# State scan of a two-layer model: y summed token-major by accumulating transposes, one eighth of u·B by PE with diagonal matrices from GpSimd

## The reference, cut to what matters

```
z       = second half of in_proj(hidden)          # 512 channels
delta   = softplus(...)                           # [token, d]
u       = delta * x_conv
h[t,d,n] = exp(delta[t,d] * A[d,n]) * h[t-1,d,n] + u[t,d] * B[t,n]
y[t,d]   = sum over n of h[t,d,n] * C[t,n]
y       = (y + x_conv * D) * silu(z)
out     = y @ out_proj.T                          # added to x
```

## Time and profile before

| | us |
|---|---|
| median of three runs | 1728.73 (1726.64 to 1728.74) |
| the profiled execution | 1728.79 |
| its span | 1727.0 |
| PE busy | 1649.3 (96%) |
| DVE busy | 1394.7 (81%) |
| ACT busy | 1267.8 (73%) |
| POOL busy | 765.0 (44%) |
| first product h·C to the end of the last, sequence 0 | 1140.15 to 1312.79 |
| the same, sequence 1 | 1386.29 to 1559.79 |

### The profile page before, as it was taken

The page is one execution under the profiler, slowest core; times in us unless marked ns, Lnnn a source line. Parts: engine busy times, 40 slices in busy tenths (PEclk is TensorE's granted clock), DMA queues, the critical chain, the costliest instruction groups (busy, mean ns, idle before and its releaser), DMA issues.

```text
span 1727.0 us, 31389 instructions
## 1 busy us (share of the span) xinstructions
PE 1649.3 (96%) x9564; PEld 1366.6 (79%) x9564; DVE 1394.7 (81%) x2319; ACT 1267.8 (73%) x2380; POOL 765.0 (44%) x717
## 2 busy tenths in 40 slices
PE   8999999999999999999997899789999899999998
PEld 7899889998999889989996788556557656557887
DVE  7788878887787778777876667878888788888997
ACT  5777777777777777777774555799996899984442
POOL 4444445443545354445442111059883079881000
PEclk9999999999999999999999999989999999999999
DMA  3000000000000000000000000023220022240000
GB/s 99 32 20 19 28 27 18 18 30 24 16 16 28 24 15 15 27 24 15 22 0 16 35 0 0 4 87 108 94 89 13 18 108 97 98 142 5 13 13 25
DMA packets 25105, 64.13 MB, mean 37 GB/s; under 512 B 2832, under 2 KB 8976, under 8 KB 24784
## 3 DMA queue, kind: packets, MB, share of 16 engines
q1 hardware_dynamic: 25040, 63.31, 10.8%
HBM read 60.94 MB, written 2.36 MB: 37 GB/s over the span
## 4 chain that ended last, share of the span: by engine, by line
PE 63%; POOL 18%; DVE 10%; issue 6%; ACT 2%; DMA 1%; POOLq 0%; DVEq 0%; SPq 0%; ACTq 0%
POOL m_h L2494 16%; PE ps L567 11%; PE ps L529 10%; PE ps L552 7%; PE ps L484 7%; PE ps L580 5%; PE ps L507 5%; PE ps L802 4%; PE ps L709 3%; PE ps L814 2%; PE ps L730 2%; POOL prob L2364 1%; PE ps L984 1%; POOL prob L2357 1%; DVE m_delta L2175 1%
## 5 line engine op out<-in xcount | busy, mean ns | idle before, releaser
L2494 POOL TENSOR_TENSOR m_h<-m_h,m_C 128x1024 f32<-128x1024 f32 x128 | 309.6, 2424 | 161.4 <-DVE m_h L2238 161.0
L2238 DVE TENSOR_TENSOR_SCAN m_h<-m_y,ps 128x1024 f32<-128x1024 f32 x128 | 291.0, 2283 | 44.9 <-PE ps L939 41.8
L2364 POOL TENSOR_SCALAR prob<-prob,rinv 128x128 f32<-128x128 f32 (+7 forms) x256 | 229.2, 903 | 212.7 <-DVE rinv L1655 206.2
L2357 POOL TENSOR_SCALAR prob<-prob 128x128 f32<-128x128 f32 (+7 forms) x256 | 188.4, 736 | 285.5 <-ACT prob L1077 277.0
L946 PE MATMUL ps<-m_h,ident 128*128 128x512 f32 x512 | 246.0, 603 | 11.2 <-POOL m_h L2494 11.1
L1621 DVE TENSOR_TENSOR pt_lo<-ps,pt_hi 128x512 fp32r<-128x512 f32 (+2 forms) x320 | 189.4, 604 | 81.0 <-ACT pt_hi L1090 79.2
L1614 DVE CUSTOM_DVE_ANT_0 prob<-prob,bias 128x128 f32<-128x128 f32 (+7 forms) x256 | 213.9, 853 | 7.9 <-POOL prob L2357 4.7
L1077 ACT ACTIVATE prob<-ps 128x128 f32<-128x128 f32 (+7 forms) x256 | 165.9, 653 | 67.2 <-PE ps L529 66.6
L1090 ACT ACTIVATE pt_hi<-ps 128x512 fp32r<-128x512 f32 (+2 forms) x320 | 162.9, 531 | 66.5 <-PE ps L552 64.5
L1464 ACT ACTIVATE m_u<-m_uT,m_bT 128x256 f32<-128x256 f32 x512 | 210.7, 497 | 0.1
L1083 ACT ACTIVATE prob<-prob,nmax 128x128 f32<-128x128 f32 (+7 forms) x256 | 198.2, 776 | 3.0 <-DVE nmax L1614 2.0
(11 more groups left out here) (263 smaller groups left out, 3960.2 us busy)
## 6 DMA issues: line engine op xcount, KB each, us to landing
m_C<-bc_dram SPq DMA_DIRECT2D x64, 512.0 KB, 3.6
wqk_raw<-wqk_in SPq DMA_DIRECT2D x16, 512.0 KB, 3.2
wv_raw<-wv_in SPq DMA_DIRECT2D x16, 256.0 KB, 2.6
wo_raw<-wo_in SPq DMA_DIRECT2D x16, 256.0 KB, 2.8
q_raw<-wgu_in SPq DMA_DIRECT2D x8, 256.0 KB, 2.7
raw<-wgu_in SPq DMA_DIRECT2D x1, 2048.0 KB, 8.1
out<-x SPq DMA_DIRECT2D x8, 256.0 KB, 2.1
x<-x_in SPq DMA_DIRECT2D x2, 512.0 KB, 4.4
```

The lines of the kernel that those rows point to most:

```text
L2238: nc.vector.tensor_tensor_scan(m_h[:, 2 * (v % 2) + e, :], m_da[:, 2 * (v % 2) + e, :], drive(e), 0.0, ALU.mult, ALU.add).then_inc(scan_do ...
L2357: nc.gpsimd.tensor_scalar(prob[:, at:at + n], prob[:, at:at + n], CLIP, -CLIP, ALU.min, ALU.max).then_inc(s_clipped, 1)
L2364: nc.gpsimd.tensor_scalar(prob[:, at:at + n], prob[:, at:at + n], rinv[:, k:k + 1], 1.0, ALU.mult, ALU.mult).then_inc(norm_done, 1)
L2494: nc.gpsimd.tensor_tensor(state, state, m_C[:, v, :], ALU.mult).then_inc(hc_done, 1)
```

## The change

1. y is summed with tokens on the partitions. `add_state` now makes eight 128x128 fp32 transposes of `m_h` a unit that accumulate in PSUM. `y_block(t, e)` gives two token tiles of 256 channels to a bank, banks 0 to 3 as before.
2. x_conv·D goes into the sum first: POOL multiplies the four chunks (`xd_done`) in place, and PE turns two chunks of the half into the accumulator (`begin_y`). DVE's `dve_mamba_skip` is gone.
3. z is made by tokens (`pe_in_z`), with as many matmuls as before, and `dve_mamba_gate` multiplies y by silu(z) in that layout, out of PSUM, in two instructions a half.
4. The gated y is turned back by eight transposes a chunk (`pe_y_turn`, new). `act_y_hi` and `dve_mamba_y_lo` read it in PSUM. For chunks 0 and 1 it lies for that time in the banks of `drive(e)`, in the second group of four states of half 1; for the others in banks that are free at the end.
5. `spread` leaves out the last of the eight token tiles. For it PE multiplies the turned u (as weights) by a diagonal matrix of B, one plain fp32 matmul of 128x128 a unit. POOL makes the 16 diagonal matrices of a sequence (`diag_b`) from the identity and `m_bT`, ahead of everything else that it does in that sequence's scan. PE waits for all 16 before its first expand.
6. At the end of each sequence PE's order is changed to fit the turns; `pe_sparse` loses a wait that is no longer needed.

```diff
@@ memory
+        m_dB = (raw_rest[:, :].rearrange("p (n q) -> p n q", q=P), m_dB1)
@@ y_block, y_bank
+        def y_block(t, e):
+            return ps[:, t // 2, (t % 2) * 2 * P + e * P:(t % 2) * 2 * P + (e + 1) * P]
+        def y_bank(b, e):
+            if e < 2:
+                return 4 + 2 * e
+            return (6, 4)[e - 2] if b < B - 1 else (2, 0)[e - 2]
@@ PE, expand and add_state
-                for t in range(TILES):
+                for t in range(TILES - 1):
...
-                mm.then_inc(db_done, 1)
-            def add_state(half, it, v, e, begin=False, end=False):
+                t = TILES - 1
+                nc.tensor.matmul(ps[:, 4 + 2 * e + t // 4, (t % 4) * P:(t % 4 + 1) * P],
+                                 m_uT[:, half, t, e * P:(e + 1) * P], m_dB[b][:, bass.ds(it * RING + v, 1), :],
+                                 start=True, stop=True).then_inc(db_done, 1)
+            def add_state(half, it, v, e, end=False):
                 pe.wait_ge(hc_done, unit(b, half, it, v, e) + 1)
-                for c in range(2):
-                    mm = nc.tensor.matmul(ps[:, 2 * e + c, :], ident[:, :],
-                                          m_h[:, 2 * (v % 2) + e, c * BANK:(c + 1) * BANK],
-                                          start=begin, stop=end)
+                for t in range(TILES):
+                    mm = nc.tensor.matmul(y_block(t, e), m_h[:, 2 * (v % 2) + e, t * P:(t + 1) * P], ident[:, :],
+                                          start=False, stop=end and e == 1 and t % 2 == 1, is_transpose=True,
+                                          skip_group_check=True)
@@ PE, half 1
+            for e in range(2):
+                expand(1, 0, 1, e)
+            pe.wait_ge(yz_done, 4 * b + 2)
+            begin_y(1)
+            for e in range(2):
+                add_state(1, 0, 0, e)
...
+            for v in range(RING):
+                if v == 2:
+                    for e in range(2):
+                        pe.wait_ge(scan_done, unit(b, 1, 1, v, e) + 3)
+                        pe_y_turn(pe, b, e)
+                        add_state(1, 1, v - 1, e)
+                for e in range(2):
+                    if v == 2:
+                        pe.wait_ge(y_lo, DT * b + e + 1)
+                    expand(1, 1, v, e)
@@ PE, after the scans
-            pe_in_x(pe, 1, range(4))
-            pe.wait_ge(y_skip, DT)
-            pe_mamba_out(pe, 0, (0, 1))
+            pe_in_x(pe, 1, range(2))
+            pe.wait_ge(yz_done, 3)
+            pe_mamba_out(pe, 0, (0, 1), range(4))
+            pe.wait_ge(yz_done, 4)
+            pe_y_turn(pe, 0, 2)
+            pe.wait_ge(m_in_read, 16 + 4)
+            pe_y_turn(pe, 0, 3)
+            pe_mamba_out(pe, 0, (0, 1), range(4, TILES))
+            pe.wait_ge(y_lo, 3)
+            pe_in_x(pe, 1, range(2, 4))
+            pe_mamba_out(pe, 0, (2,))
+            pe.wait_ge(y_lo, 4)
             pe_in_x(pe, 1, range(4, 8))
-            pe_mamba_out(pe, 0, (2,))
             pe_mamba_out(pe, 0, (3,))
             pe_mamba_pre(pe, 1)
             pe_mamba_scan(pe, 1)
-            pe.wait_ge(y_skip, 2 * DT - 1)
+            pe.wait_ge(yz_done, 8)
+            pe_y_turn(pe, 1, 2)
+            pe_y_turn(pe, 1, 3)
+            pe.wait_ge(y_lo, 8)
             pe_sparse_turn(pe, 0)
@@ DVE
-        def dve_mamba_skip(dve, b, e):
...
+            dve.wait_ge(y_added, 8 + (2 * b + half + 1) * HALF_UNITS)
+            nc.vector.tensor_tensor(m_yT[:, half, 4 * c:4 * c + 4, :],
+                                    ps[:, 2 * c:2 * c + 2, :].rearrange("p a (t n) -> p (a t) n", t=2),
+                                    m_zT[:, half, 4 * c:4 * c + 4, :], ALU.mult).then_inc(yz_done, 1)
@@ POOL
         def pool_mamba_scan(pool, b):
+            pool.wait_ge(bt_read, b + 1)
+            pool.wait_ge(m_bc_out, 16 * (b + 1))
+            for n in range(DN):
+                nc.gpsimd.tensor_scalar(m_dB[b][:, n, :], ident[:, :], m_bT[:, TILES - 1, n:n + 1], None,
+                                        ALU.mult).then_inc(diag_b, 1)
+            for e in range(DT):
+                pool.wait_ge(m_sp, 5 * DT * b + 3 * DT + 2 * e + 2)
+                nc.gpsimd.tensor_scalar(m_xc[:, e, :], m_xc[:, e, :], skip_d[:, e:e + 1], None,
+                                        ALU.mult).then_inc(xd_done, 1)
```

More of the change, by code:

```diff
@@ L953, in pe_mamba_scan @@
+            last = DN // RING - 1
+            pe.wait_ge(diag_b, DN * (b + 1))
+            for e in range(2):
+                expand(0, 0, 0, e)
+            begin_y(0)
+            for v in range(1, RING):
                 for e in range(2):
-                    expand(half, 0, 0, e)
-                    if half:
-                        add_state(0, last, RING - 1, e, end=True)
-                for v in range(1, RING):
+                    expand(0, 0, v, e)
+                    add_state(0, 0, v - 1, e)
@@ L958, in pe_mamba_scan @@
+            with pe.Fori(1, last + 1) as it:
+                for v in range(RING):
                     for e in range(2):
[L959 to L970 removed]
+                        expand(0, it, v, e)
+                        if v:
+                            add_state(0, it, v - 1, e)
+                        else:
+                            add_state(0, it - 1, RING - 1, e)
@@ L971, in pe_mamba_scan @@
+            with pe.Fori(2, last + 1) as it:
+                for v in range(RING):
+                    for e in range(2):
+                        expand(1, it, v, e)
+                        if v:
+                            add_state(1, it, v - 1, e)
+                        else:
+                            add_state(1, it - 1, RING - 1, e)
             for e in range(2):
```

126 lines of the change are left out of this document (69 added, 57 removed).

## The result

The changed kernel takes 1730.55 us (median of 20 runs, 1728.93 to 1733.73), the kernel before 1728.01 (20 runs, 1726.04 to 1728.93). The ratio is 1.0017, with a 95% interval of 1.0011 to 1.0023: slower by 2.5 us between the medians, about the 0.2% that the prediction took for no change. Forecast were 1709.5 us and a range of 1700 to 1724. The profiled execution of the changed kernel took 1733.5 us, 2.9 above its median, with a span of 1731.7.

A forecast was written before the change was run, and what follows sets the result against it. Four engines within 15%, PE and ACT equally late in the steady scan; afterwards ACT at 2.43 us a unit, POOL just behind. Scans -12.2 and -12.7, between sequences +2.3, end +3.4: -19.2, from 1728.7 to 1709.5 us; range 1700 to 1724.

The forecast's parts named there:

- one scan along POOL: Sequence 0's scan counted along POOL: 1141.5 + 151.7 + 7.4 = 1300.6, 12.2 us earlier; sequence 1 12.7 earlier.
- start: Scan start: diagonals 6.05 us, blocking 1.4, products with D 4.5; first product at 1141.5, 1.3 us later than before.
- over 3: Sign of being wrong, at the scan's start: PE late by more than 3 us.
- Steady part: Steady scan: PE's unit 2.0 us, ACT 4.86 a pair (2.43 a unit) as next bound, POOL 2.37.
- 161 us: Sign in the trace after: both scans 161 us long.
- Idle of POOL: POOL's waits in a scan: 1.2 us after the first pair, 1.9 at change of half, 4.3 at the turn; sum 7.4.
- Between the sequences: From sequence 0's last product into sequence 1's convolution: +2.3 us, bounds 0.5 and 5.
- after sequence 1: From sequence 1's last product to the weights' low parts done: +20.7 us, so +3.4; bounds 2 and 7.
- The ring: Rival, steady scan: the engines' waiting ring grows and sets 2.45 to 2.53 us a unit; 1716 to 1723; chance 0.20.
- The edges' rival: Rival: scan faster, but diagonals, turns and second end cost upper bounds (+5, +3, +4 and blocking); 1722 to 1729; chance 0.08.
- The clock: Rival: PE falls to 1.2 GHz in the scans; about 1910 throughout, 1750 to 1760 half the time; chance 0.11.
- The same: Outcome of no change in the whole program's time, within 0.2% (3.5 us): chance 0.05.

The follow-up runs named there:

- the two-operation kernel: Changed kernel with POOL's diagonals and products with D both written with two operations (also "the kernel with both edits"): 1710.47 us, ratio to before 0.9896.
- the kernels with one or both edits: Changed kernel with two operations on the diagonals alone (1722.05 us), on the products with D alone (1714.53 us), or on both (1710.47 us).

## Why the prediction was wrong, by its own steps

**The step that failed** is in "one scan along POOL", under start: "16 diagonals of 0.378, 6.05 us" and "the four products with D are 4.5 us more". They took 10.30 and 11.31. That is 11.1 us more. I had added 1.4 for blocking by DVE (it took 0.7, and is in the 10.30), so 9.7 us were not covered. From the end of `m_bT` to the first product it was 10.6 us before, forecast 11.9 and is 21.7: 9.7 us over the forecast, and the same in sequence 1. PE's first expand comes 10.5 us after `m_bT` where it came after 6.1, 4.4 late, and over 3 was one of the signs named for being wrong. The mechanism (POOL's prelude ahead of its first product) was right; the sizes were taken from rows of another form of the instruction. The earlier trace rows show products of two operations, the second a multiplication by 1.0; the new lines have `None`. I read the line number, the shape and the type, and not the operands in the code. With the same instructions written in the form that was priced, and nothing else changed, the kernel takes 1710.5 us; the forecast was 1709.5. That it is so near is in part luck, as the next paragraphs show.

**The bounds failed with it.** For a form that the trace didn't show I gave a bound only for the diagonals, twice the row and PE 7 us late, and it would have held. The products with D had none, and they are the larger part of the miss, 6.8 us of the 11.1. The nearest row beside the earlier trace rows was POOL's own product of two tensors, 2.37 us; as an upper bound for them it would have given +5 us a sequence, 1719.5, and would still have been short of 2.84.

**Steady part.** Right. Unit 2.32 to 2.34 us, adds 0.93 of issue for eight accumulating transposes (0.88 forecast), ACT 4.87 a pair (4.86), gaps of PE for POOL behind each add. In the changed kernel POOL, late by its prelude, goes at its own pace and ACT has the lead; ACT's pace shows only once the prelude is short. The plain fp32 product was over-priced: 0.23 us of issue in the trace of the two-operation kernel (1142.80 to 1143.03), against the 0.35 that I took. From first to last product the changed kernel needs 160.2 and 159.7 us, against 151.7 + 7.4 = 159.1. (The "161 us" among the prediction's signs does not follow from its own sum.) Two misses offset each other in that: products in a row follow each other every 2.34 us and not 2.37, so 64 take 149.5 in place of 151.7, and POOL's idle time is 10.7 and 10.2 in place of 7.4.

**Idle of POOL.** Under-counted by some 3 us a sequence. In sequence 0: at the change of half 2.07 and 0.28 us (1.9), at the turn 4.64 (4.3), then 1.42 more, which I had not counted. The start lost 1.79 and 0.49 us (1.2). In sequence 1 there is nothing behind the turn, but 1.44 us later on, where DVE puts its statistics of the rows (1.7 us) between two scans; the kernel before has that wait too. The new gates and low parts cost POOL nothing, as taken: three products beside them are 7.04 us.

```profile
1227.72 7.04 POOL L2584 TENSOR_TENSOR m_h<-m_h,m_C 128x1024 f32<-128x1024 f32 x3
...
1232.22 2.33 DVE L2359 TENSOR_TENSOR m_xc<-ps,m_z 128x1024 f32<-128x1024 f32 x2
...
1236.83 4.71 POOL L2584 TENSOR_TENSOR m_h<-m_h,m_C 128x1024 f32<-128x1024 f32 x2 [2.07 <-DVE m_h L2332]
```

**Between the sequences** +2.1 us (2.3), **after sequence 1** +3.8 (3.4). Both right within 0.4 us, the second down to PE's stop of 4.35 us (4.4).

**The rivals.** The ring did not grow. The edges' rival was about such an end, but by other terms: edges at their upper bounds (+5, +3 and +4). Between the sequences and at the end they kept to their forecast, and the loss came by the prelude alone. The clock held in the steady part, which the windows of the changed kernel show (stretch, length, PE busy, PEclk, DMA share, GB/s):

```profile
1140.00:1160.00 20.00, 12.19 (x64) 0.67 0.05 18
1200.00:1240.00 40.00, 35.55 (x295) 1.00 0.30 108
1260.00:1280.00 20.00, 15.62 (x121) 0.91 0.22 79
```

In the steady part PE is busy 35.55 of 40 us with little but transposes, and the granted clock is 1.00, that is 2.4 GHz. The other two stretches are means over time at 1.00 and time at 0.50, that is 1.2 GHz, and both have stops in them: at the start waits of 6.91 and 5.83 us, at the turn one of 1.34 and one of 1.23. By the rule of the Trainium skill that the prediction weighed (TensorE: Matmul & The Clock Gate, section Part 4: PE-mode transpose), it would have been low throughout; the measurement decides against it here.

What the clock does cost is at the turn. In sequence 0 of the changed kernel it falls to 0.50 in the second stop, at about 1267, and is back at about 1270.5; the add behind it takes 1.97 us in place of 1.09, and POOL has its 1.42 us of wait. In sequence 1 of the kernel with both edits PE has the same two stops (1.36 and 1.23 us) and the same fall, and POOL waits 1.53. In the changed kernel's sequence 1 the clock stays at 1.00 through the turn, and so it does in sequence 0 of the kernels with one or both edits; there POOL's wait is absent. So the fall costs about 1.4 us each time, and one and the same program has it in one sequence and not in the other.

**The chances.** "The same" had 0.05 and the edges' rival 0.08. Both were too low, since the range reached only as far as my own prices: the 4.5 us for the products with D stood in the sum without an upper bound, so that their being dear was in no chance at all.

## What to carry to other kernels

A price from the trace holds for the instruction with its operands as written, not for the engine, the name and the shape; where the new code differs in a single operand from the row that it is priced by, the instruction is timed by itself first. The next dearer row on that engine is no safe bound: here it was 2.37 us, and the product took 2.84. On GpSimd an fp32 product by one number a partition is written with two operations (times it, times 1.0); in this program that was cheaper at every width from 128 to 1024 columns. And where two engines are equally late, each half of a change can be worth nothing or less alone, as here: price the pair, then read the new bound before working on the edges that it hides.
